# The last 128 KB of output in one transfer of 128 partitions, or in two of 64 from two queues

## The reference

```
x = x + lora(x)      # x W_base^T + b + 2 * sum over 8 experts of cond_8 * (x A^T) B^T
x = x + moe(x)       # top 2 of 8 experts by softmax(cond_8), and a shared one:
                     # (gelu(x Wg) * (x Wu)) Wd, hidden width 512
x = x + expert(x)    # the expert argmax(cond_8): (silu(x Wu^T + bu) * (x Wg^T + bg)) Wd^T + bd, width 256
x = x + masked(x)    # x (sum over g of cond_8[g] * weight[g] * mask)^T + bias
```

## Time and profile before

| | |
|---|---|
| device time, median of 3 runs | 72.99 us (72.33 to 73.17) |
| the profiled execution's own time | 72.82 us |
| its span, first to last instruction | 71.5 us |
| granted TensorE clock | 1.00 |
| TensorE, VectorE, ScalarE, GpSimd busy | 95%, 64%, 68%, 51% |
| DMA moved | 6.62 MB, of it 0.52 MB written |

### The profile page before, as it was taken

One profiled execution on the slowest core, in us unless ns is written; L12 is line 12 of the kernel. 1 busy time (PEld: TensorE's weight loads), 2 busy tenths in 40 slices (PEclk: granted clock), 3 DMA queues, 4 the chain that ended last, 5 costly groups with the idle time before them and its releaser, 6 DMA issues.

```text
span 71.5 us, 1068 instructions
## 1 busy us (share of the span) xinstructions
PE 67.8 (95%) x316; PEld 55.0 (77%) x316; DVE 45.6 (64%) x83; ACT 48.7 (68%) x96; POOL 36.4 (51%) x50
## 2 busy tenths in 40 slices
PE   4998999999999999999999999999999999999950
PEld 4996868788788788788788787787788788788640
DVE  0256778577655567765556775555986576958960
ACT  0736879466787666678666668869678995674660
POOL 3020573054999999866999986655540700000000
DMA  0797899999500000000000000000000000000017
GB/s 1 195 373 277 296 393 370 423 419 410 225 0 9 0 0 0 0 0 0 5 5 0 0 0 0 0 0 9 0 0 0 0 0 0 0 0 0 0 39 254
DMA packets 2884, 6.62 MB, mean 93 GB/s; under 512 B 448, under 2 KB 1728, under 8 KB 2880
## 3 DMA queue, kind: packets, MB, share of 16 engines
q1 hardware_dynamic: 2304, 6.05, 22.4%
q10 hardware_dynamic: 576, 0.52, 2.2%
HBM read 6.04 MB, written 0.52 MB: 92 GB/s over the span
## 4 chain that ended last, share of the span: by engine, by line
PE 94%; DVE 1%; ACT 1%; issue 1%; DVEq 0%
PE gp L432 9%; PE gp L428 9%; PE gp L429 9%; PE acc L432 9%; PE acc L428 9%; PE acc L429 9%; PE up L432 9%; PE up L428 9%; PE up L429 9%; PE up L409 4%; PE up L577 1%; PE acc L457 1%; PE acc L424 1%; PE gp L538 1%; PE gp L415 1%; ACT xhi L333 1%
## 5 line engine op out<-in xcount | busy, mean ns | idle before, releaser
L355 ACT ACTIVATE act<-gp 128x512 f32<-128x512 f32 x24 | 14.4, 600 | 11.8 <-PE gp L432 11.5
L264 POOL TENSOR_TENSOR wlo<-raw_skill,whi 128x384 fp32r<-128x384 f32 x16 | 16.3, 1018 | 7.8 <-ACT whi L328 7.7
L641 DVE TENSOR_TENSOR hlo<-up,hhi 128x512 fp32r<-128x512 f32 x27 | 18.4, 682 | 1.9 <-ACT hhi L343 1.9
L634 DVE SCALAR_TENSOR_TENSOR up<-up,gate_w,act 128x512 f32<-128x512 f32 x16 | 12.1, 759 | 11.1 <-ACT act L355 11.0
L343 ACT ACTIVATE hhi<-up 128x512 fp32r<-128x512 f32 x27 | 16.0, 594 | 2.8 <-DVE up L627 2.6
L428 PE MATMUL acc<-hhi,whi 128*128 128x512 f32 (+1 forms) x28 | 11.2, 401 | 0.0
L428 PE MATMUL gp<-xhi,whi 128*128 128x512 f32 x27 | 11.2, 414 | 0.0
L432 PE MATMUL acc<-hlo,whi 128*128 128x512 f32 (+1 forms) x28 | 10.9, 388 | 0.0
L429 PE MATMUL acc<-hhi,wlo 128*128 128x512 f32 (+1 forms) x28 | 10.8, 387 | 0.0
L428 PE MATMUL up<-xhi,whi 128*128 128x512 f32 x27 | 10.7, 396 | 0.0
L432 PE MATMUL up<-xlo,whi 128*128 128x512 f32 x27 | 10.7, 396 | 0.0
(11 more groups left out here) (109 smaller groups left out, 93.3 us busy)
## 6 DMA issues: line engine op xcount, KB each, us to landing
raw_skill<-skill SPq DMA_DIRECT2D x4, 768.0 KB, 6.6
raw_shared<-shared SPq DMA_DIRECT2D x4, 192.0 KB, 3.8
w3in<-l SPq DMA_DIRECT2D x1, 576.0 KB, 5.6
raw_l<-l SPq DMA_DIRECT2D x1, 386.5 KB, 7.6
raw_l<-l_folded SPq DMA_DIRECT2D x1, 386.5 KB, 7.5
x<-x_t ACTq DMA_DIRECT2D x2, 128.0 KB, 3.3
x<-x_t SPq DMA_DIRECT2D x1, 256.0 KB, 4.2
out_t<-res SPq DMA_DIRECT2D x1, 256.0 KB, 2.0
```

The costliest lines, as they stand in the source:

```text
L264: pool.tensor_tensor(wlo[:, p, c], raw_piece(p)[:, c], whi[:, p, c], ALU.subtract).then_inc(s_wlo, 1)
L355: sc.activation(act[:, k % 2, :], gp[k % PAIRS][:, :], ACT.Gelu_apprx_tanh).then_inc(s_act, 1)
L634: ve.scalar_tensor_tensor(out=out, in0=u, scalar=gate_w[:, b, r:r + 1], in1=a, op0=ALU.mult, op1=ALU.mult).then_inc(s_h, 1)
L641: ve.tensor_tensor(hlo[:, i, t], hidden_of(k, t), hhi[:, i, t], ALU.subtract).then_inc(s_hlo, 1)
```

## The change

The store of the last half of batch 1 is cut in two by partitions. SyncE stores partitions 0 to 63; ScalarE, after its own store of the first half, waits for the same semaphore of VectorE and stores partitions 64 to 127. The bytes and the rows of 1 KB are the same in all. Each transfer adds 16 to `s_out`, so the last wait is for 64 in place of 48.

```
                 sp.wait_ge(s_res1[1], 1)
-                sp.dma_start(out_t[:, T + HALF:], res[:, 1, HALF:]).then_inc(s_out, 16)
+                sp.dma_start(out_t[:P // 2, T + HALF:], res[:P // 2, 1, HALF:]).then_inc(s_out, 16)
...
                 sc.dma_start(out_t[:, T:T + HALF], res[:, 1, :HALF]).then_inc(s_out, 16)
+                sc.wait_ge(s_res1[1], 1)
+                sc.dma_start(out_t[P // 2:, T + HALF:], res[P // 2:, 1, HALF:]).then_inc(s_out, 16)
...
         def stores_have_landed(sp):
-            sp.wait_ge(s_out, 16 * 3)
+            sp.wait_ge(s_out, 16 * 4)
```

## The result

The changed kernel takes 73.65 us (median of 22 runs, 72.77 to 75.84) against 72.90 us (median of 22 runs, 72.24 to 73.70). The ratio is 1.0087, with a 95% interval of 1.0058 to 1.0116: about 0.6 us slower. Taken once more beside other kernels, the ratio was 1.0054 (1.0009 to 1.0098).

A forecast was written before the change was run, and what follows sets the result against it. TensorE was taken to own 94% of the span, with a bare 1.9 us DMA tail at its end. Terms 0 + 0 + 0.03 + 0.01 = +0.04 us on the 72.99 us median gave 73.0 us, range 72.5 to 73.45.

The forecast's parts named there:

- Within 1%: Outcome class for the changed kernel's time against the kernel before: a difference of at most 1%, chance 0.92.
- the sum: All priced steps of the tail added: 0 + 0 + 0.03 + 0.01 = +0.04 us, giving 73.0 us.
- The issue of 64 partitions: SyncE's last store, halved to 64 KB: issue left at 0.35 us, first packet possible 0.85 us after issue, gain none.
- The cover: At the tail, ScalarE's data is needed at 70.79 and can be there at 70.49, hiding its late issue by 0.30 us.
- The second transfer: ScalarE's added store, issued 0.04 us behind SyncE's: late issue covered with 0.30 us to spare, cost none.
- rival 2: Last two stores share one descriptor generator; second's first packet 0.85 us after the first's: +0.4 us, 73.4 us; chance 0.04.
- Rival 1: Last stores: 64 partitions reach half the DMA read path, packets up to 96 ns: +0.1 to +0.38 us, chance 0.22.
- the 0.27 us estimated beside it: Estimate from the Trainium skill for the last stores: 128 KB at 196 in place of 328 GB/s costs 0.27 us more.
- The completions: Final wait, 64 counts in place of 48: 16 more small packets, +0.01 us, bounds nothing to 0.14 us.
- Rival 3: Last store's halves run side by side and halve its data time: -0.19 us, -0.2 with queue overlap, 72.8 us; chance 0.09.
- this rule: Trainium skill on two transfers to disjoint partition halves: not to bother, both use the same 16 engines; change gives 0.
- Rival 4: ScalarE's second store issue stalls until its first store completes: +1.6 us, 74.6 us; chance 0.01.

## Why the prediction was wrong, step by step

The forecast was 73.0 us with a range to 73.45, and 73.65 was measured. "Within 1%" held (ratio 1.0087), but the loss is real, and in the tail, at 0.39 us, ten times the sum's 0.04 us. The bound of the kernel and of the tail was read rightly: the first two stores fill the DMA engines, and nothing ahead of the tail was shown to change. Two small readings in the working are off and decide nothing: q10 has 120 + 24 = 144 packets in the earlier trace rows, not 143, and the 0.39 us at the lower end of ScalarE's next issue has no row (0.41 was measured).

- **The issue of 64 partitions, the step that failed first.** The prediction left it "at 0.35", because 256 and 128 KB took the same. Those rows varied the bytes of 128 partitions, not the number of partitions, so they bounded nothing for the new shape, and no upper end was given. Measured: 0.53 to 0.58 us wherever 64 partitions are moved, and a first packet 1.19 us after the issue in place of a possible 0.85. The cover, the backlog of the first two stores, thins out 1.0 us after the issue, so a hole opened. At the end the cuts at 80 and 96 put about 0.14 us on it.
- **The second transfer, "covered with 0.30 us to spare".** The sum has "Cost: none" for it. Its first packet, allowed for at 0.89 us after SyncE's issue and needed by 1.19, came at 1.47. It starts 0.28 us after the first. The runs with tiny transfers of 64 partitions and with ScalarE held back bear out the mechanism of rival 2, a second transfer that waits for the first without data in its way; its price of 0.85 us was too high by a factor of three. With tiny transfers of 128 partitions the gap is 0.09 us, inside the cover. The prediction had bounded it at 0.1 to 0.2 us from the earlier trace rows and hidden it under the cover; but the cover had been worked out for data that starts at 0.85 and 1.0 us, and with both late it was gone. This is the larger part, up to 0.25 us: it stays in the cuts at 80 and 96, where the second transfer starts 0.27 and 0.36 us after the first. Those also have slow packets in the first transfer, and how the 0.25 divides between late start and slow packets there is not separated; cut by columns, two transfers cost 0.15.
- **Rival 1, the paths of neighbouring partitions.** Right as a mechanism: 65 to 68 ns a packet, and 186 for 2 KB. Its price, forecast at 0.1 to 0.38, is 0.11 us at the last packet and 0.02 us at the end, as the even and odd partitions show; the 0.27 us estimated beside it was too high as well. Its sign, slow packets with busy engines at little over half the rate, stood in the profile as described, and taken by itself it would have been the wrong story; only spreading the partitions showed it.
- **The completions.** Priced at 0.01; nothing in the runs speaks for more.
- **Rival 3** is excluded: the last half's data ends later, not earlier. No gain was right, but the 0 that stands there for this rule is too good: the tail grew by 0.39 us. **Rival 4** as well: ScalarE issues again 0.41 us after its first issue.
- **The chances.** The mechanisms were weighed as alternatives. They were not: the long issue, the late second transfer and the slow packets happened at once, and the first took the cover that the second was to hide under. That rivals 1 and 2 each forecast about the 0.39 us that the tail grew by is chance: rival 1's slow packets were worth 0.02 us at the end, and rival 2 had the second part's first packet at 1.70 us after the issue, where it came at 1.47.

What stays open: from the last data to the end of the span it is 0.38 to 0.39 us before and after the change, but 0.42 and 0.47 in the cuts at 80 and 96, 0.44 in that by columns, 0.47 with even and odd partitions and 0.61 with the tiny transfers of 128. The runs don't say why, so a part of what these cuts cost is not explained by issue or packets. The tail explains 0.39 us, and the first comparison's interval, 0.42 to 0.85 us, begins just above that; the second's, 0.07 to 0.71, holds it. Since the start of an execution moves by more than the difference, whether something beyond the tail is lost can't be told from these profiles.

## What to carry to other kernels

A transfer of this size at the end costs issue, first packet and landing far more than bytes: half of the data saved 0.08 us in the old shape, and in a new shape it ended later than all of it in the old one. All five ways of cutting this last store over two queues lengthened the tail; the cut that kept all 128 partitions in each part lost least (0.15 us), 64 neighbouring partitions most (0.39). And when a step is said to be hidden, redo the cover with the late values of the other unknown steps, not with their best ones.

## What was not expected of the hardware

- A transfer of 64 partitions takes 0.53 to 0.58 us to issue, neighbouring or every second one, 64 bytes to 2 KB a row; 128, 96 and 80 partitions take 0.35 to 0.36, and 48 and 32, issued second by ScalarE, 0.45, which 128 partitions take there too (0.46). Right behind two issues of 64 partitions, one of 128 took 0.59.
- Two issues of 64 partitions at one moment on SyncE and ScalarE bring their first packets 0.27 us apart, with the DMA engines nearly idle; of 128 partitions with rows of 64 bytes, 0.09 us apart.
- With 64 bytes a row in place of 512 to 1024, the tail of two transfers is only 0.14 us (columns) to 0.29 us (64 partitions) shorter.
